# Four graph layers in a row: the middle product of the last three works on rows, with split operands, and every queue has a new order

## The chip, the core and the metric

The kernel runs on one core of a Trainium2 chip. A core has five engines that run side by side, each its own queue of instructions in a fixed order: TensorE (PE in the profile, with PEld for its weight loads), VectorE (DVE), ScalarE (ACT), GpSimd (POOL), and SyncE (SP), which here issues all transfers. They meet through semaphores: an instruction waits until a counter has reached a value that another engine's instruction raises. The metric is the time of one execution on the device in microseconds, as the median of several runs.

## The reference

The input is 128 small graphs of 128 nodes with 256 features each (`x`), and one weighted adjacency matrix of 128 x 128 for each (`adj`). Four blocks follow one another. Each takes `h = relu(layernorm(x))` and adds its result to `x`:

```python
x = x + L0(h, adj)   # hypergraph convolution 256 -> 512, relu, layer norm, 512 -> 256, residual
x = x + L1(h, adj)   # tanh(norm(adj) @ (h W) + b), with ones on the diagonal of adj != 0
x = x + L2(h, adj)   # attention: exp(leaky(8 tanh(score/8))) * adj, its sums, then (A h) w
x = x + L3(h, adj)   # three layers adj @ (x W) + b, relu after the first and the second
```

In L3, with A the adjacency matrix of one graph:

```python
x1 = relu(A @ (h  @ W1) + b1)
x2 = relu(A @ (x1 @ W2) + b2)
out =     A @ (x2 @ W3) + b3
```

Everything is computed in 32-bit precision or close to it. Since A @ (x W) = (A @ x) W, each layer may mix nodes first or weigh first.

## The kernel before, in words

**Streams and steps.** The 128 graphs go through in 16 groups of 4 streams (A, B, C, D) of J = 2 graphs each. Per stream and group there are the same steps, each named by block and kind. On PE a step `nU` ("unit") multiplies a graph's features with its 128 x 128 matrix, and a step `nW` ("weigh") multiplies with the layer's weights: `0U 0W 1U 1W` are L0, `2U 2W` L1, `3S 3U 3W` L2 (`3S` spreads the scores), and `4U 4W 5U 5W 6U 6W` L3. `G` forms the product of the incidence matrices.

**Two ways to multiply.** `unit` (L308) uses plain f32 products: the rows H (128 nodes x 256 features) are the stationary operand in two halves, the matrix of 128 x 128 moves through, so that the result lies in PSUM with features on the partitions, which is what the weighing needs as its stationary operand. There are two graphs and two halves, so four products of 128 x 128 a step; the trace counts each f32 product as two matmuls. `weigh` (L334) splits both operands in a high part rounded to fp32r and a low part (the rest), and adds three products, W low x U high, W high x U high, W high x U low: with 256 inputs and two graphs these are 12 fp32r matmuls, each of 256 moving columns.

**What the other engines do for one layer of L3.** After `4U`, ScalarE copies the bank rounded to fp32r (`take`, L435, tile UHI), VectorE subtracts that from the bank (`low`, L576, tile ULO), PE weighs (`4W`), VectorE adds the bias (`biased`, L618, tile H), ScalarE applies relu (`relu`, L483), and `5U` starts on H. `5U 5W` and `6U 6W` go the same way; `6W` ends in `last_out` on VectorE and a transfer.

**Around it.** GpSimd turns variances into scales (`norm`, L705 a power), prepares residuals, and in `with_loops` (step `AT`, L718 and L721) makes L1's matrix: incidences times a mask without diagonal, plus the identity. ScalarE's `normalise` (L404), `scores_tanh` (L470) and `scores_exp` (L477, L478), VectorE's `stats` (L535), `hidden` (L593), `leak`, `attend` and `attention_sums` (L624 to L635) serve the other blocks.

**PSUM.** Two wide pairs of banks serve `0W`, `1U` and the setup; four single banks serve all other PE steps in rotation. `bank_free` makes a step wait until the step four single-bank users earlier has been read by the engines named in `FREED`.

**Order.** The order of each queue is written out in full in `ORDER`, as three lists per engine: a first part, one turn that repeats, a last part. `ordered` numbers the occurrences of a step: the n-th is stream n modulo 4 and group n // 4. PE's turn has 16 steps; different steps of one turn belong to different streams, so that while one stream waits for ScalarE and VectorE the others keep PE at work. PE's first and last parts hold 73 and 72 steps. The SP queue loads and stores in the same manner: `T` loads the matrix for the next group once `6U` has read it, `R` the untransposed matrix, `O` stores a result.

## Time and profile before

| | |
|---|---|
| median of 3 runs | 1349.94 us (1349.46 to 1351.4) |
| the profiled execution | 1351.4 us |
| its span, first to last instruction | 1349.6 us |
| busy: PE, DVE, ACT, POOL | 1326.8, 1182.8, 1048.1, 1056.1 us |
| mean granted TensorE clock | 0.997 of full speed |
| DMA | 64.48 MB, 48 GB/s on the mean |

The span is shorter than the time of the execution by what lies before the first and behind the last instruction. Busy times are those of the profiled execution alone. A matmul's end is modelled and overlaps the start of the next; so a PE at 98% is one that is hardly ever without work, and what its work costs is better read from the distance between two starts. The same holds in a small measure for neighbours on ScalarE and VectorE.

### The profile page before, as it was taken

The numbers are of one execution on the slowest core, as the hardware profiler recorded it, in microseconds if no ns is written. First come the engines' busy times: TensorE is split into PE (matmuls) and PEld (weight loads), VectorE is DVE, ScalarE is ACT, GpSimd is POOL, SyncE is SP. The second block draws the span as 40 slices with busy tenths as digits, with TensorE's granted clock in tenths as the row PEclk, the third lists the DMA queues.
The fourth block names the chain that finished last, engine by engine and source line by source line (L and its number), as shares of the span: only waits on it lengthen the run. The fifth ranks groups of instructions, "written<-read, shape, count | busy, mean of one in ns | idle before, by whom it ended". The sixth has DMA issues, their size and how long they took to land.

```text
span 1349.6 us, 32286 instructions
## 1 busy us (share of the span) xinstructions
PE 1326.8 (98%) x10680; PEld 1282.2 (95%) x10680; DVE 1182.8 (88%) x3607; ACT 1048.1 (78%) x2632; POOL 1056.1 (78%) x2004
## 2 busy tenths in 40 slices
PE   8899999999999999999999999999999999999988
PEld 7889999999999999999999999999999999999987
DVE  8878898898998898898898898998998998989875
ACT  6776877887887887887887877877877877878864
POOL 7876778778788788788788788788788888888761
PEclk9989999999999999999999999999999999999999
DMA  7011111111111111111111111111111111111100
GB/s 215 21 32 33 44 57 37 48 56 37 48 56 37 48 56 37 48 56 37 48 56 37 48 56 36 49 53 39 49 50 39 52 48 37 56 48 33 33 9 32
DMA packets 83220, 64.48 MB, mean 48 GB/s; under 512 B 40304, under 2 KB 65520, under 8 KB 83056
## 3 DMA queue, kind: packets, MB, share of 16 engines
q1 hardware_dynamic: 83056, 62.43, 15.8%
q8 instruction: 87, 1.43, 0.4%
q14 instruction: 77, 0.63, 0.2%
HBM read 45.62 MB, written 16.78 MB: 46 GB/s over the span
## 4 chain that ended last, share of the span: by engine, by line
PE 89%; DVE 6%; ACT 2%; issue 1%; POOL 1%; DVEq 0%; POOLq 0%; ACTq 0%
PE BANK L351 29%; PE BANK L319 24%; PE BANK L358 14%; PE WIDE L330 8%; PE WIDE L351 8%; PE WIDE L358 4%; PE BANK L304 2%; PE BANK L369 1%; DVE BN_D L535 0%; DVE BN_B L535 0%; DVE BN_A L535 0%; DVE BN_C L535 0%; DVE ULO_B L576 0%; DVE ULO_A L576 0%; ACT H_B L404 0%
## 5 line engine op out<-in xcount | busy, mean ns | idle before, releaser
L576 DVE TENSOR_TENSOR ULO_D<-BANK,UHI_D 128x512 fp32r<-128x512 f32 x96 | 65.6, 684 | 18.6 <-ACT UHI_D L435 18.5
L576 DVE TENSOR_TENSOR ULO_B<-BANK,UHI_B 128x512 fp32r<-128x512 f32 x96 | 65.6, 683 | 17.5 <-ACT UHI_B L435 17.4
L576 DVE TENSOR_TENSOR ULO_A<-BANK,UHI_A 128x512 fp32r<-128x512 f32 x96 | 65.6, 683 | 17.0 <-ACT UHI_A L435 17.0
L576 DVE TENSOR_TENSOR ULO_C<-BANK,UHI_C 128x512 fp32r<-128x512 f32 x96 | 65.5, 683 | 14.1 <-ACT UHI_C L435 14.1
L435 ACT ACTIVATE UHI_C<-BANK 128x512 fp32r<-128x512 f32 x96 | 57.4, 598 | 21.3 <-PE BANK L319 20.1
L435 ACT ACTIVATE UHI_B<-BANK 128x512 fp32r<-128x512 f32 x96 | 57.3, 597 | 20.5 <-PE BANK L319 19.1
L435 ACT ACTIVATE UHI_A<-BANK 128x512 fp32r<-128x512 f32 x96 | 57.4, 598 | 19.5 <-PE BANK L319 18.1
L435 ACT ACTIVATE UHI_D<-BANK 128x512 fp32r<-128x512 f32 x96 | 57.3, 597 | 18.7 <-PE BANK L319 17.4
L705 POOL TENSOR_TENSOR LN_D<-LN_D,MHALF 128x2 f32<-128x2 f32 x80 | 55.7, 696 | 1.3
L705 POOL TENSOR_TENSOR LN_A<-LN_A,MHALF 128x2 f32<-128x2 f32 x80 | 55.7, 696 | 1.3
L705 POOL TENSOR_TENSOR LN_C<-LN_C,MHALF 128x2 f32<-128x2 f32 x80 | 55.6, 695 | 1.3
L705 POOL TENSOR_TENSOR LN_B<-LN_B,MHALF 128x2 f32<-128x2 f32 x80 | 55.6, 695 | 1.3
L404 ACT ACTIVATE H_B<-RES_B,LN_B 128x256 f32<-128x256 f32 x96 | 52.4, 600 | 5.1 <-POOL LN_B L713 5.0
L404 ACT ACTIVATE H_C<-RES_C,LN_C 128x256 f32<-128x256 f32 x96 | 52.4, 599 | 4.6 <-POOL LN_C L713 4.6
L404 ACT ACTIVATE H_A<-RES_A,LN_A 128x256 f32<-128x256 f32 x96 | 52.4, 599 | 3.9 <-POOL LN_A L713 3.9
L404 ACT ACTIVATE H_D<-RES_D,LN_D 128x256 f32<-128x256 f32 x96 | 52.3, 598 | 2.4 <-POOL LN_D L713 2.4
L319 PE MATMUL BANK<-T_B,H_B 128*128 128x128 f32 x384 | 51.7, 278 | 0.6 <-ACT H_B L483 0.6
L319 PE MATMUL BANK<-T_C,H_C 128*128 128x128 f32 x384 | 50.8, 275 | 0.5 <-ACT H_C L483 0.5
L319 PE MATMUL BANK<-T_A,H_A 128*128 128x128 f32 x384 | 50.7, 275 | 0.4 <-ACT H_A L483 0.4
L319 PE MATMUL BANK<-T_D,H_D 128*128 128x128 f32 x384 | 50.9, 275 | 0.2
L319 PEld LDWEIGHTS BANK<-T_B,H_B 128*128 128x128 f32 x384 | 48.6, 194 | 2.2 <-ACT H_B L483 0.8
L319 PEld LDWEIGHTS BANK<-T_D,H_D 128*128 128x128 f32 x384 | 47.8, 191 | 2.0 <-ACT H_D L483 0.7
(487 smaller groups left out, 5761.5 us busy)
## 6 DMA issues: line engine op xcount, KB each, us to landing
X_A<-in_xs SPq DMA_DIRECT2D x16, 256.0 KB, 2.5
X_B<-in_xs SPq DMA_DIRECT2D x16, 256.0 KB, 2.7
X_C<-in_xs SPq DMA_DIRECT2D x16, 256.0 KB, 2.6
X_D<-in_xs SPq DMA_DIRECT2D x16, 256.0 KB, 2.6
out_rows<-O_A SPq DMA_DIRECT2D x16, 256.0 KB, 2.0
out_rows<-O_B SPq DMA_DIRECT2D x16, 256.0 KB, 2.0
out_rows<-O_C SPq DMA_DIRECT2D x16, 256.0 KB, 2.1
out_rows<-O_D SPq DMA_DIRECT2D x16, 256.0 KB, 2.0
```

Of the source, the lines that this page charges most:

```text
L304: last = nc.tensor.matmul(bank(s, "G", k)[:, j * (P + 2):(j + 1) * (P + 2)], HT[s][:, j, :], BHT[s][:, j, :], start=True, stop=True)
L319: last = nc.tensor.matmul(bank(s, step, k)[:, at:at + P], lhs[s][:, j, m * P:(m + 1) * P], rhs(s, j), start=True, stop=True)
L330: last = nc.tensor.matmul(bank(s, "1U", k)[:, j, m * P:(m + 1) * P], Z[s][:, j, m * P:(m + 1) * P], GZ[s][:, j, :], start=True, stop=True)
L351: nc.tensor.matmul(dst, UHI[s][:, at[m]:at[m] + P], w[:, m, :], start=(w is lo and m == 0), stop=False)
L358: last = nc.tensor.matmul(dst, ULO[s][:, at[m]:at[m] + P], hi[:, m, :], start=False, stop=(m == chunks - 1))
L369: last = nc.tensor.transpose(bank(s, "3S", k)[:, j * P:(j + 1) * P], ST[s][:, S8, j:j + 1].to_broadcast([P, P]), IDENT[:, :])
L404: nc.scalar.activation(dst[s][:, j, :], src[s][:, j, :], ACT.Relu, bias=LN[s][:, NB, j:j + 1], scale=LN[s][:, RSTD, j:j + 1]).then_inc(sem ...
L435: nc.scalar.activation(UHI[s][:, 0:J * D], bank(s, step, k)[:, :], ACT.Copy).then_inc(sem(f"c{step}"), 1)
L576: nc.vector.tensor_tensor(ULO[s][:, 0:J * D], bank(s, step, k)[:, :], UHI[s][:, 0:J * D].bitcast(F32), ALU.subtract).then_inc(sem(f"l{step ...
L705: nc.gpsimd.tensor_tensor(rstd, ve, MHALF[:, :], ALU.pow)\
```

## The change

The middle layer of L3 now weighs first and mixes nodes afterwards; `4W` leaves its result with features on the partitions, so that `5W` can take it as the stationary operand without a `5U` in between.

- `4U` and its copy are laid out in pairs (`paired`): both graphs' columns side by side for each half of the features.
- `4W` is `weigh_columns`: the weights are stationary and 256 columns of UHI or ULO (two graphs x 128 nodes) move. 12 fp32r matmuls as before.
- ScalarE adds bias 1, now a column L3B1C, and applies relu in place in PSUM in two halves (`relu_columns`, step `4W`), then copies the bank to UHI (`take_columns`, step `4V`); VectorE subtracts (`low`, step `4V`).
- `5W` weighs with W2 from there; ScalarE copies and VectorE subtracts its result (steps `5W`).
- `5U` is `unit_rows`: the matrix T, split in THI and TLO, is stationary; the rows of UHI and ULO (256 columns) move. Per graph three fp32r matmuls, six in all. Then VectorE adds bias 2 (`biased`, step `5U`), ScalarE applies relu (`relu_rows`, step `5U`), and `6U`, `6W` are as before.
- THI is a rounded copy by ScalarE (`TH`), TLO the rest by GpSimd (`TL`).
- `with_loops` writes ones on the diagonal with two selections (`affine_select`) in place of a product and a sum; the mask OFFDIAG is gone.
- A user of a bank after `3S` also waits for `ae_ready`. The raw weights of `6W` have a tile of their own. Bias 1 is loaded as a column by one transfer, no longer spread over the partitions.
- All five orders are new, first and last parts too (left out below; PE's hold 73 and 72 steps again, and its turn is repeated 55 times in both kernels).

```diff
 ORDER = {
     "PE": (
...
-         "0U 4W 3S 0W 5U 2U 3U 5W 2W 3W G 6U 1U 1W 4U 6W",
...
+         "0U 4W 3S 0W 2U 5W 3U 2W 5U 3W G 6U 1U 1W 4U 6W",
...
     "ACT": (
...
-         "3W 2X 4U 2Y 0U 3T 4W 3E 1W SH 5U 2U 0W 3U R B 5W 2W 0Z H0 1U G 6U",
...
+         "G 1U 3W 2X TH 4U 2Y 0U SH 4W 4V 3T 1W 3E R 2U 0W 5W 3U B H0 5U 2W 0Z 6U",
...
     "DVE": (
...
-         "X XA 3L 3E 3R 0W 5U 2U 0S 3U 3I 0A 3J 5W 2W 3W 3S 3A 2S 2A 1U DA DB 6U T DC 1W 4U 1S DD 1A 0U 4W 6W",
...
+         "XA 4V 0W 3L 3E 3R 2U 0S 5W 3U 3I 0A 5U 2W 3J 3W 3S 3A 2S 2A 1U T DA DB X 6U DC 1W 1S 4U DD 1A 0U 6W",
...
     "POOL": (
...
-         "RX RB NZ 2A N3 N2 RH 2N DI AT N1 TB N0 X3",
...
+         "RB NZ 2A N3 N2 RH 2N AT TB N1 DI N0 RX TL X3",
...
     "SP": (
...
-         "W R F D O X T",
...
+         "D W O T F X R",
...
         B1 = sb("B1", [P, DH])
-        B2, L1B, L3B1, L3B2, L3B3 = (sb(n, [P, D]) for n in ("B2", "L1B", "L3B1", "L3B2", "L3B3"))
-        BIAS = {"4W": L3B1, "5W": L3B2}
+        B2, L1B, L3B2, L3B3 = (sb(n, [P, D]) for n in ("B2", "L1B", "L3B2", "L3B3"))
+        L3B1C = sb("L3B1C", [P, DC])
         BW = sb("BW", [P, D])
...
         IDENT = sb("IDENT", [P, P])
-        OFFDIAG = sb("OFFDIAG", [P, P])
         ONES = sb("ONES", [P, P])
...
         R = per_stream("R", J, P)
+
+        THI = per_stream("THI", J, P, dt=F32R)
+        TLO = per_stream("TLO", J, P, dt=F32R)
...
         L2WT = TMP["D"]
-        RAW = {"0W": W1, "1W": W2, "2W": O["A"], "3W": O["B"], "4W": O["C"], "5W": O["D"], "6W": H["D"]}
+        RAW = {"0W": W1, "1W": W2, "2W": O["A"], "3W": O["B"], "4W": O["C"], "5W": O["D"], "6W": sb("RAW6W", [P, DC, D])}
...
                 sp.dma_start(RAW[step][:, :, :], src).then_inc(sem(f"raw_loaded_{step}"), 16)
-            for dst, src in ((L1B, l1b), (L3B1, l3b1), (L3B2, l3b2), (L3B3, l3b3)):
+            for dst, src in ((L1B, l1b), (L3B2, l3b2), (L3B3, l3b3)):
                 sp.dma_start(dst[:, :], src.partition_broadcast(P)).then_inc(sem("bias_loaded"), 16)
+            column = bass.AP(l3b1.tensor, l3b1.offset, [[1, P], [P, DC], [1, 1]])
+            sp.dma_start(L3B1C[:, :].unsqueeze(2), column, allow_slow_non_contiguous=True).then_inc(sem("bias_column"), 16)
             for s in STREAMS[1:]:
...
             FREED = {"G": "cG", "3S": "sums_done", **{step: f"l{step}" for step in U_STEPS}, **{step: f"c{step}" for step in W_STEPS},
-                     "4W": "b4W", "5W": "b5W", "shifts": "w2c_ready"}
+                     "4W": "l4W", "5W": "l5W", "5U": "b5U", "shifts": "w2c_ready"}
             FREED_BY = {"c0W": J, "l1U": J, "c1W": J, "c2W": J, "c3W": J}
...
                     pe.wait_ge(sem(FREED[step0]), FREED_BY.get(FREED[step0], 1) * done_at(s0, k0))
+                    if step0 == "3S":
+                        pe.wait_ge(sem("ae_ready"), done_at(s0, k0))
...
-            def unit(step, lhs, rhs, *signals, rows=None):
+            def unit(step, lhs, rhs, *signals, rows=None, paired=False):
                 def f(s, c, k):
...
                         for m in range(DC):
-                            at = j * D + m * P
+                            at = (m * J + j) * P if paired else j * D + m * P
                             last = nc.tensor.matmul(bank(s, step, k)[:, at:at + P], lhs[s][:, j, m * P:(m + 1) * P], rhs(s, j),
...
-            def weigh(step):
+            def weigh_columns(s, c, k):
+
+                hi, lo = WHI["4W"], WLO["4W"]
+                if k == 0:
+                    pe.wait_ge(sem("weights_split"), W_STEPS.index("4W") + 1)
+                pe.wait_ge(sem("c4U"), c["n1"])
+                bank_free(s, "4W", k)
+                n = J * P
+                for q in range(DC):
+                    dst = bank(s, "4W", k)[:, q * n:(q + 1) * n]
+                    for w in (lo, hi):
+                        for m in range(DC):
+                            nc.tensor.matmul(dst, w[:, m, q * P:(q + 1) * P], UHI[s][:, m * n:(m + 1) * n],
+                                             start=(w is lo and m == 0), stop=False)
+                    if q == 0:
+                        pe.wait_ge(sem("l4U"), c["n1"])
+                    for m in range(DC):
+                        last = nc.tensor.matmul(dst, hi[:, m, q * P:(q + 1) * P], ULO[s][:, m * n:(m + 1) * n], start=False,
+                                                stop=(m == DC - 1))
+                last.then_inc(sem("p4W"), 1)
+
+            def unit_rows(s, c, k):
+
+                pe.wait_ge(sem("tl_ready"), c["n1"])
+                pe.wait_ge(sem("c5W"), c["n1"])
+                bank_free(s, "5U", k)
+                for j in range(J):
+                    dst, rows = bank(s, "5U", k)[:, j * D:(j + 1) * D], slice(j * D, (j + 1) * D)
+                    nc.tensor.matmul(dst, TLO[s][:, j, :], UHI[s][:, rows], start=True, stop=False)
+                    nc.tensor.matmul(dst, THI[s][:, j, :], UHI[s][:, rows], start=False, stop=False)
+                    if j == 0:
+                        pe.wait_ge(sem("l5W"), c["n1"])
+                    last = nc.tensor.matmul(dst, THI[s][:, j, :], ULO[s][:, rows], start=False, stop=True)
+                last.then_inc(sem("p5U"), 1)
+
+            def weigh(step, of=None, paired=False):
+                of = of or f"{step[0]}U"
                 chunks, n = WIDTH[step]
...
                         pe.wait_ge(sem("weights_split"), W_STEPS.index(step) + 1)
-                    pe.wait_ge(sem(f"c{step[0]}U"), c["v"][0] if step == "1W" else c["n1"])
+                    pe.wait_ge(sem(f"c{of}"), c["v"][0] if step == "1W" else c["n1"])
                     bank_free(s, step, k)
...
                         dst = to[:, j, :] if step == "0W" else to[:, j * n:(j + 1) * n]
-                        at = [j * chunks * P + m * P for m in range(chunks)]
+                        at = [(m * J + j if paired else j * chunks + m) * P for m in range(chunks)]
                         if step == "1W" and j:
...
                         elif j == 0:
-                            pe.wait_ge(sem(f"l{step[0]}U"), c["n1"])
+                            pe.wait_ge(sem(f"l{of}"), c["n1"])
                         for m in range(chunks):
...
                 "3U": unit("3U", H, lambda s, j: AE[s][:, j, :], "ae_ready"),
-                "4U": unit("4U", H, lambda s, j: T[s][:, j, :], rows="h3_ready"),
-                "5U": unit("5U", H, lambda s, j: T[s][:, j, :], "c4W"),
-                "6U": unit("6U", H, lambda s, j: T[s][:, j, :], "c5W"),
-                **{step: weigh(step) for step in W_STEPS}}
+                "4U": unit("4U", H, lambda s, j: T[s][:, j, :], rows="h3_ready", paired=True),
+                "5U": unit_rows,
+                "6U": unit("6U", H, lambda s, j: T[s][:, j, :], "c5U"),
+                **{step: weigh(step) for step in W_STEPS}, "4W": weigh_columns, "5W": weigh("5W", of="4W", paired=True)}
             run("PE", parts)
...
-            def relu(step):
-                def f(s, c, k):
-                    act.wait_ge(sem(f"b{step}"), c["n1"])
-                    nc.scalar.activation(H[s][:, :, :], H[s][:, :, :], ACT.Relu).then_inc(sem(f"c{step}"), 1)
-                return f
+            def relu_rows(s, c, k):
+                act.wait_ge(sem("b5U"), c["n1"])
+                nc.scalar.activation(H[s][:, :, :], H[s][:, :, :], ACT.Relu).then_inc(sem("c5U"), 1)
+
+            def relu_columns(s, c, k):
+
+                if k == 0:
+                    act.wait_ge(sem("bias_column"), 16)
+                act.wait_ge(sem("p4W"), c["n1"])
+                for q in range(DC):
+                    half = bank(s, "4W", k)[:, q * J * P:(q + 1) * J * P]
+                    last = nc.scalar.activation(half, half, ACT.Relu, bias=L3B1C[:, q:q + 1])
+                last.then_inc(sem("r4W"), 1)
+
+            def take_columns(s, c, k):
+                act.wait_ge(sem("r4W"), c["n1"])
+                nc.scalar.activation(UHI[s][:, 0:J * D], bank(s, "4W", k)[:, :], ACT.Copy).then_inc(sem("c4W"), 1)
+
+            def high_t(s, c, k):
+                act.wait_ge(sem("t_loaded", s), c["dma"])
+                nc.scalar.activation(THI[s][:, :, :], T[s][:, :, :], ACT.Copy).then_inc(sem("th_ready"), 1)
...
                      "2X": normalise(RES, H, "ln2_ready", "h2_ready"), "2Y": node_scores, "3T": scores_tanh, "3E": scores_exp,
-                     "3U": take("3U"), "3W": normalise(RES, H, "ln3_ready", "h3_ready"), "4U": take("4U"), "4W": relu("4W"),
-                     "5U": take("5U"), "5W": relu("5W"), "6U": take("6U")}
+                     "3U": take("3U"), "3W": normalise(RES, H, "ln3_ready", "h3_ready"), "4U": take("4U"), "4W": relu_columns,
+                     "4V": take_columns, "5W": take("5W"), "5U": relu_rows, "6U": take("6U"), "TH": high_t}
             run("ACT", parts)
...
                 if k == 0:
-                    dve.wait_ge(sem("bias_loaded"), 4 * 16)
+                    dve.wait_ge(sem("bias_loaded"), 3 * 16)
                 dve.wait_ge(sem("dinv"), c["n1"])
...
-            def biased(step):
-                def f(s, c, k):
-                    dve.wait_ge(sem(f"p{step}"), c["n1"])
-                    rows = bank(s, step, k)[:, :].rearrange("p (j d) -> p j d", j=J)
-                    nc.vector.tensor_tensor(H[s][:, :, :], rows, pair(BIAS[step][:, :]), ALU.add).then_inc(sem(f"b{step}"), 1)
-                return f
+            def biased(s, c, k):
+                dve.wait_ge(sem("p5U"), c["n1"])
+                rows = bank(s, "5U", k)[:, :].rearrange("p (j d) -> p j d", j=J)
+                nc.vector.tensor_tensor(H[s][:, :, :], rows, pair(L3B2[:, :]), ALU.add).then_inc(sem("b5U"), 1)
...
                      "3I": sums_inverse, "3J": sums_ratio, "3W": attention_out, "3S": stats(RES, "3", "c3W"),
-                     "3A": aggregate("3"), "4W": biased("4W"), "5W": biased("5W"), "6W": last_out, **{step: low(step) for step in U_STEPS}, "1U": low_hidden}
+                     "3A": aggregate("3"), "6W": last_out, **{step: low(step) for step in U_STEPS}, "1U": low_hidden, "4V": low("4W"), "5W": low("5W"),
+                     "5U": biased}
             dve.wait_ge(sem("ones_ready"), 1)
...
                                     pattern=[[-1, P]], channel_multiplier=1).then_inc(sem("ident_ready"), 1)
+            pool.wait_ge(sem("mhalf_ready"), 1)
             pool.wait_ge(sem("ident_ready"), 1)
-            nc.gpsimd.tensor_tensor(OFFDIAG[:, :], ONES[:, :], IDENT[:, :], ALU.subtract).then_inc(sem("offdiag_ready"), 1)
-            pool.wait_ge(sem("mhalf_ready"), 1)
-            pool.wait_ge(sem("offdiag_ready"), 1)
...
                 pool.wait_ge(sem("ht_ready"), c["n1"])
-                nc.gpsimd.tensor_tensor(AT[s][:, :, :], HT[s][:, :, :], pair(OFFDIAG[:, :]), ALU.mult)\
-                    .then_inc(sem("at_offdiag"), 1)
-                pool.wait_ge(sem("at_offdiag"), c["n1"])
-                nc.gpsimd.tensor_tensor(AT[s][:, :, :], AT[s][:, :, :], pair(IDENT[:, :]), ALU.add).then_inc(sem("at_ready"), 1)
+                for j in range(J):
+                    last = nc.gpsimd.affine_select(out=AT[s][:, j, :], in_=HT[s][:, j, :], compare_op=ALU.not_equal, fill=1.0, base=0,
+                                                   pattern=[[-1, P]], channel_multiplier=1)
+                last.then_inc(sem("at_ready"), 1)
...
+            def low_t(s, c, k):
+                pool.wait_ge(sem("th_ready"), c["n1"])
+                nc.gpsimd.tensor_tensor(TLO[s][:, :, :], T[s][:, :, :], THI[s][:, :, :].bitcast(F32), ALU.subtract)\
+                    .then_inc(sem("tl_ready"), 1)
+
             def last_bias(s, c, k):
                 if k == 0:
-                    pool.wait_ge(sem("bias_loaded"), 4 * 16)
+                    pool.wait_ge(sem("bias_loaded"), 3 * 16)
                 pool.wait_ge(sem("h3_ready"), c["v"][J - 1])
...
                      "NZ": norm("z"), "N1": norm("1", DINV), "2A": gcn_add, "N2": norm("2"), "2N": weighted, "N3": norm("3"),
-                     "X3": last_bias}
+                     "X3": last_bias, "TL": low_t}
             run("POOL", parts, per_pass=(1, 4))
```

## Rows read from the trace of the kernel before

**Rows 1.** The page's part 1: busy us of each engine, share of the span, instructions

```profile
PE 1326.8 (98%) x10680; PEld 1282.2 (95%) x10680; DVE 1182.8 (88%) x3607; ACT 1048.1 (78%) x2632; POOL 1056.1 (78%) x2004
```

**Rows 2.** Stretches; busy us of PE, weight loads, DVE, ACT, POOL; PE clock, DMA share, GB/s

```profile
65.00:70.00 5.00, 2.47 (x14) 2.26 (x13) 4.48 (x17) 4.39 (x12) 4.49 (x12) 0.78 0.00 0
...
80.00:85.00 5.00, 4.49 (x23) 4.30 (x24) 3.61 (x14) 3.68 (x10) 4.77 (x12) 0.66 0.02 3
...
sum 130.00, PE 118.01 PEld 109.99 DVE 106.06 ACT 88.92 POOL 97.58; mean PE 4.54 PEld 4.23 DVE 4.08 ACT 3.42 POOL 3.75
...
200.00:400.00 200.00, 200.00 (x1636) 194.58 (x1635) 180.64 (x552) 160.43 (x403) 162.61 (x308) 1.00 0.15 45
...
sum 130.00, PE 118.79 PEld 111.44 DVE 97.66 ACT 86.02 POOL 77.89; mean PE 4.57 PEld 4.29 DVE 3.76 ACT 3.31 POOL 3.00
```

**Rows 3.** The chain of waits, mid-body: start us, us, what

```profile
465.23 1.79 PE WIDE L330 x16
...
485.53 1.79 PE WIDE L330 x16
```

**Rows 4.** PE's timeline in one turn: start us, us, instructions

```profile
697.65 0.71 PE L351 MATMUL WIDE<-WLO0W,UHI_C 128*128 128x512 f32 x2
...
700.54 1.05 PE L319 MATMUL BANK<-T_D,H_D 128*128 128x128 f32 x8
701.43 1.06 PE L319 MATMUL BANK<-AT_B,H_B 128*128 128x128 f32 x8
702.32 1.06 PE L319 MATMUL BANK<-AE_A,H_A 128*128 128x128 f32 x8
703.13 0.48 PE L351 MATMUL BANK<-WLO5W,UHI_D 128*128 128x256 f32 x2
703.46 0.39 PE L351 MATMUL BANK<-WHI5W,UHI_D 128*128 128x256 f32 x2
...
704.59 0.39 PE L351 MATMUL BANK<-WLO2W,UHI_B 128*128 128x256 f32 x2
```

**Rows 5.** ScalarE's timeline in the same turn

```profile
698.51 0.63 ACT L483 ACTIVATE H_D<-H_D 128x512 f32<-128x512 f32 x1
699.03 0.39 ACT L477 ACTIVATE BANK<-AE_A 128x256 f32<-128x256 f32 x1
699.34 0.41 ACT L478 ACTIVATE AE_A<-AE_A 128x256 f32<-128x256 f32 x1
699.65 1.09 ACT L404 ACTIVATE H_B<-RES_B,LN_B 128x256 f32<-128x256 f32 x2
```

**Rows 6.** VectorE's timeline in the same turn

```profile
699.94 0.41 DVE L624 TENSOR_TENSOR BANK<-BANK,AE_A 128x256 f32<-128x256 f32 x1
...
701.21 1.41 DVE L593 SCALAR_TENSOR_TENSOR Z_C<-WIDE,ST_C,B 128x512 f32<-128x512 f32 x2
702.53 0.68 DVE L576 TENSOR_TENSOR ULO_D<-BANK,UHI_D 128x512 fp32r<-128x512 f32 x1
...
703.76 1.28 DVE L535 BATCH_NORM_STATS2 BN_C<-Z_C 128x6 f32<-128x512 f32 x2
```

**Rows 7.** Groups by line: busy us, mean ns of one, idle before them

```profile
L435 ACT ACTIVATE UHI_A<-BANK 128x512 fp32r<-128x512 f32 x96 | 57.4, 598 | 19.5 <-PE BANK L319 18.1
...
L618 DVE TENSOR_TENSOR H_A<-BANK,L3B 128x512 f32<-128x512 f32 x32 | 22.0, 689 | 4.0 <-PE BANK L358 3.2
...
L718 POOL TENSOR_TENSOR AT_A<-HT_A,OFFDIAG 128x256 f32<-128x256 f32 x16 | 11.7, 734 | 1.7 <-DVE HT_A L549 1.7
...
L687 POOL TENSOR_SCALAR_AFFINE_SELECT IDENT<-IDENT 128x128 f32<-128x128 f32 x1 | 0.3, 292 | 0.2 <-POOL IDENT L685 0.2
```

**Rows 8.** Timelines of ScalarE and PE in the last turns

```profile
1337.80 0.63 ACT L483 ACTIVATE H_C<-H_C 128x512 f32<-128x512 f32 x1 [0.73 <-DVE H_C L618]
...
1338.48 1.16 PE L319 MATMUL BANK<-T_C,H_C 128*128 128x128 f32 x8 [0.20 <-ACT H_C L483]
...
1344.31 0.50 PE L351 MATMUL BANK<-WLO6W,UHI_D 128*128 128x256 f32 x2 [0.69 <-ACT UHI_D L435]
```

55 rows, old and new, of the table ORDER are left out of this document.

## The prediction

> **What bounds the kernel now.** The page's first part comes first: TensorE (PE) is busy for 98% of the span, VectorE 88%, ScalarE and GpSimd 78% each [rows 1]. An average over stages says little, so the next view is the busy time of each engine by stretch. From 200 to 400 us PE is busy without a break, at the full granted clock (the 2.4 GHz level); in the same 200 us VectorE works 180.6, ScalarE 160.4 and GpSimd 162.6 [rows 2]. The idle time of PE lies at the two ends: 12.0 us in the first 130, 11.2 in the last 130. Two stretches of the beginning also show PE at a reduced clock, 0.78 and 0.66 on the mean of 5 us (part of each at the 1.2 GHz level), just after it had stood idle; that costs some (0.22 + 0.34) x 5 = 2.8 us. The third view is the chain of waits: in the middle it holds nothing but PE, and the same instruction comes back after 485.53 - 465.23 = 20.30 us [rows 3]. That is one turn of the written order, and the body repeats it 55 times before and 55 times after (64 less the `0U` written out in first and last part). So a microsecond taken from PE's turn is worth 55 to 64, and one taken from another engine nothing, as long as its results come in time.
>
> The fourth view is PE's timeline, and here start-to-start times count, not the mean of one: matmuls overlap in the pipeline, and the modelled 0.39 or 1.05 us of a group reaches into the next [rows 4].
>
> **The change, part by part.**
>
> *5U multiplies split operands (`unit_rows`).* Before, `5U` was four f32 products of 128 x 128, which the trace counts as 8 matmuls: 701.43 - 700.54 = 0.89 us [rows 4]. After, it is 6 fp32r matmuls that move 256 columns. Of a 5W's 12 such matmuls, the ten behind the first pair take 704.59 - 703.46 = 1.13, so one is 0.113 and six are 0.68. Gain 0.21 us. Passing from f32 to fp32r: the last f32 group before it takes 0.81 instead of 0.89 (702.32 to 703.13), the first pair 0.33 instead of 0.23, together 0.02 more. A turn has five such places before (ahead of 4W, 0W, 5W, 1W, 6W) and six after (2W now follows 3U), so 0.02 is lost. Net 0.19 a turn.
>
> The Trainium skill, "TensorE: Matmul & The Clock Gate", section "Back-to-back issue gap", gives a warm gap of N/2.4 + 2.5 ns, 109 ns at 256 columns. By that the six would take 0.66, and the sum below would be 1.6 us better. The rows' 113 decides here.
>
> *4W and 5W.* 4W keeps 12 matmuls with 256 moving columns; only which operand is stationary changes (`weigh_columns`). 5W keeps its 12. Cost nothing on PE: both forms load 128 columns of weights for 256 moving ones.
>
> *ScalarE.* Before, this layer pair took two relus of 128x512 (0.63 us each by their row) and the eviction of 5U; after: two halves of 128x256 with the bias (`relu_columns`), an eviction of them (`take_columns`), an eviction of 5W, one relu, and `TH`, a copy of 128x256. From start to start ScalarE needs 0.31 us for a 128x256, into PSUM or not (699.03, 699.34, 699.65), and 0.52 for a 128x512 (698.51) [rows 5]; I take that for the evictions too. Added: 2 x 0.31 + 0.52 + 0.31, removed one relu 0.52, and an estimated 0.1 for the wait on its own halves: +1.0 us a turn. By the full durations it is 2 x 0.39 + 0.60 + 0.41 - 0.63 = 1.16. ScalarE's load goes from 80% to about 85% of a turn; nothing on the path as long as it is below PE. A column bias read from PSUM back into PSUM is not in the trace: from below 0.31, from above the 0.60 of a full 128x512 eviction (598 ns, [rows 7]), so 0 to 0.6 us a turn more. I take 0.31, the row nearest in size.
>
> *VectorE.* Two bias additions (689 ns [rows 7]) and `5U`'s low part (0.68 us [rows 6]) become the low parts of 4W and 5W and one bias addition: the same count at the same price, 0.
>
> *GpSimd.* `with_loops` loses two operations of 128x256 (734 ns and its like), and gains two selections of 128x128. One selection of that size took 0.3 us, 292 ns, in the setup [rows 7]. `TL` adds one subtraction of 128x256, 0.73. Sum: 0.58 + 0.73 - 1.47 = -0.15; if a selection costs as much as the 734 of a whole pair, +0.73. GpSimd has 19% free. Covered; 0. Loading a bias as a column (256 small pieces) is one DMA in place of a broadcast, needed only at the first 4W, some 70 us in: 0.
>
> *The new places in the order.* Do results still come in time? I lay one turn of the new PE order against the queues, time 0 at the end of 0W, which takes 700.54 - 697.65 = 2.89 [rows 4]. PE: 4W ends at -3.0, 2U 0.9, 5W 2.3, 3U 3.2, 2W 4.6, then 5U to 5.3, 3W to 6.6, G, 6U from 7.1. ScalarE from -2.9: 4W, 4V, 3T, 1W, 3E, R, 2U, 0W, 5W, nine parts of 0.5 to 1.0, some 6.0 in all: its take of 5W is done at 3.1. VectorE: second half of 0W until 0.7 (a pair takes 1.32 [rows 6]), leak, attend and sums 1.27 (699.94 to 701.21), low 2U 0.61 (two lows: 702.53 to 703.76), then 0S 1.2, low 5W: done near 4.4. 5U wants that low part only after its first two matmuls, at 4.8: 0.4 to spare. Its bias and relu end near 6.6 for a 6U at 7.1: 0.5 to spare. The narrowest is 6U's bank, freed by VectorE's 2W at about 6.85: 0.25. All positive, so the turn stays PE's and is 20.30 - 0.19 = 20.11.
>
> *The last turns.* Before, PE waits at the end for pairs of bias and relu: from the start of ScalarE's relu to the dependent 5U are 1338.48 - 1337.80 = 0.68, and the last 6W starts 0.69 after PE fell idle [rows 8]; with the low parts some 2.2 us are lost in the last 14. In the new order D's 6U still waits for bias and relu (1.6 less C's 6U, 0.89: 0.7 us), while C's 6W covers the take before D's 6W. That is 1.5 better; I take 1.0. For the beginning I find no reason of either sign and take 0: bounds are -8 (idle and slow clock there, less what the first loads need) and +6 (another wait with a slow stretch behind it). The tail's bounds are -5 and +4.
>
> **Sum.** 64 x 0.19 = 12.2, plus 1.0: span 1349.6 - 13.2 = 1336.4. The profiled execution took 1351.4, 1.8 more than its span; so 1338.2. The median of the runs is 1.46 below the profiled one, so **1336.7 us**.
>
> **Rivals.**
> - *A queue becomes late in each turn* (slower side). Place: the low part of 5W or the release of 6U's bank. Speaking for it: three queues are now 81 to 91% full, each in fixed order, and the slack found above is 0.25 to 0.5 us; a column relu at the 0.60 bound eats 0.6 of ScalarE's. Against: ScalarE is not the latest of the two at 5U (3.1 against 4.4), and before, with VectorE just as full, PE never waited. A wait of w costs 55w: at w = 0.24 all is gone, at 0.35 the time is 1336.7 + 19 = 1356. Chance of slower 0.08, of within the noise 0.08, of a small wait that leaves a gain (1342) 0.08.
> - *The new order mends the ends*: half of the idle and slow time at both ends goes, 6 us more: 1331. For it: every list of the first part is new, and setup work on VectorE is placed later. Against: new waits on ScalarE there. Chance 0.12.
> - *The ends get worse* by 5: 1342. For it: PE stood idle, and then ran at the lower level, after a single late result; ScalarE has 1 us more per stream. Chance 0.08.
> - *The split product isn't cheaper*: if each of the six had to wait for its own weights for longer than it runs, 0.19 us each where PE's own pace is 0.113 (an estimate: nearest above is the f32 product's 0.22, four in 0.89), 5U would be 1.13, 0.26 worse than before a turn: 1366. Against: 5W's twelve load as often and start every 0.113. Chance 0.01.
> - The forecast itself, 1333 to 1341: 0.55.
>
> A difference of 0.2% (2.7 us) is what a measurement of this kernel can tell from none. Faster: 0.55 + 0.12 + 0.08 + 0.08 = 0.83; within: 0.08; slower 0.09. Range 1329 to 1346.
>
> **What would show it.** A turn of 20.1 us in the chain of waits and PE busy without a break from 200 to 1200; six fp32r matmuls of `unit_rows` in 0.68; the relu halves near 0.39; PE's list of waits without VectorE's ULO or H in the middle. Wrong would be: a turn of 20.3 or more, with idle time before 5U or 6U, or clearly more idle time than 12.0 and 11.2 us in the first and the last 130.

## The result, and the profile after

The changed kernel takes 1375.85 us (median, 1375.02 to 1376.55) against 1350.67 (1349.46 to 1354.02) for the kernel before on the same chip: ratio 1.0182, 95% interval 1.0168 to 1.0196. It is slower; the forecast was 1336.7. Its profiled span is 1373.2 us against 1349.6.

Part 1 of the page after, in the columns of [rows 1]:

```profile
PE 1348.1 (98%) x10552; PEld 1293.4 (94%) x10552; DVE 1202.0 (88%) x3607; ACT 1112.6 (81%) x2824; POOL 1037.1 (76%) x2067
```

PE has 128 instructions fewer and 21.3 us more of busy time. ScalarE gained 64.5 us, about what was forecast, GpSimd lost 19, twice the forecast, and neither is full. The stretches that answer to [rows 2], same columns (stretch, its length, then the busy times):

```profile
0.00:130.00 130.00, 117.59 (x822) 108.92 (x823) 102.04 (x320) 92.91 (x228) 92.34 (x196) 0.97 0.25 72
200.00:400.00 200.00, 199.60 (x1590) 192.72 (x1590) 180.25 (x545) 165.18 (x421) 154.89 (x308) 1.00 0.16 46
1243.20:1373.20 130.00, 119.20 (x936) 113.14 (x934) 101.67 (x285) 93.35 (x233) 80.09 (x157) 1.00 0.11 33
```

The ends are as before (118.01 and 118.79 of PE there), and in the middle PE still looks full at the full clock. Busy time does not show the loss: modelled ends of matmuls overlap and cover short waits. The chain of waits does. The rows that answer to [rows 3] are the same matmuls of `0W`, one turn apart:

```profile
401.71 0.93 PE WIDE L394 x4
...
422.44 0.93 PE WIDE L394 x4
```

A turn takes 20.73 us instead of 20.30. With the 55 turns of the body this is nearly the whole loss: from the first turn's start to the last one's end there are 1140.9 us, before 1118.1, so +22.8. The first part is 2.5 longer, the last 1.7 shorter.

To see which step of the turn grew, I took the time from each step's first matmul to the next step's first, median over the turns between 200 and 1200 us (microseconds; "6U" is followed by `1U` in both kernels; e3 to e15 are experiments told below; steps that hardly moved are left out):

| step | before | after | e3 | e6 | e14 | e15 |
|---|---|---|---|---|---|---|
| 6W | 1.503 | **1.802** | 1.511 | 1.498 | 1.498 | 1.458 |
| 1W | 2.848 | 2.919 | 2.957 | 2.931 | 2.933 | 2.934 |
| 4W | 1.462 | 1.520 | 1.519 | 1.499 | 1.497 | 1.468 |
| 5W | 1.456 | 1.495 | 1.495 | 1.460 | 1.460 | 1.460 |
| 3W | 1.362 | 1.413 | 1.413 | 1.382 | 1.418 | 1.418 |
| 2W | 1.360 | 1.513 | 1.512 | 1.499 | 1.500 | 1.501 |
| 6U | 0.891 | 0.929 | 0.929 | 0.959 | 0.925 | 0.891 |
| 5U | 0.892 | 0.700 | 0.700 | 0.724 | 0.692 | 0.692 |
| 2U | 0.893 | 0.809 | 0.808 | 0.809 | 0.809 | 0.809 |

(`2U` and `2W` belong together: `2U` now stands ahead of fp32r matmuls and so ends 0.08 sooner, `2W` stands behind f32 ones and starts 0.10 slower; that is the passage of the forecast, 0.02 net.) 5U gave its 0.19. Two things ate it: **6W waits** 0.30 a turn, and **each step of 256-column matmuls is slower**, 0.27 a turn in all: 1W 0.07, 2W with 2U 0.05 net of the passage, 3W 0.05, 4W 0.06, 5W 0.04. With 0.04 at 6U and 0.02 for the passage: -0.19 + 0.30 + 0.27 + 0.04 + 0.02 = +0.44.

**The wait.** PE's timeline of the kernel after, in one turn (start us, us):

```profile
708.27 0.48 PE L394 MATMUL BANK<-WLO6W,UHI_C 128*128 128x256 f32 x2
708.59 0.39 PE L394 MATMUL BANK<-WHI6W,UHI_C 128*128 128x256 f32 x2
709.03 0.50 PE L401 MATMUL BANK<-WHI6W,ULO_C 128*128 128x256 f32 x2
709.37 0.40 PE L394 MATMUL BANK<-WLO6W,UHI_C 128*128 128x256 f32 x2
```

VectorE's, just ahead of that. `DA` (L615, L616) and `DB` (L621) prepare node degrees and their inverses, on two elements each, `X` (L594) is the statistics of the input, and L635 is the low part of `6U`:

```profile
706.43 1.09 DVE L615 TENSOR_SCALAR ST_C<-G_C 128x2 f32<-128x2 f32 x1
707.44 0.15 DVE L616 SCALAR_TENSOR_TENSOR ST_C<-DIAG_C,G_C 128x2 f32<-128x2 f32 x1
707.56 0.17 DVE L621 RECIPROCAL ST_C<-ST_C 128x2 f32<-128x2 f32 x1
707.64 0.75 DVE L594 BATCH_NORM_STATS2 BN_D<-X_D 128x6 f32<-128x256 f32 x2
708.31 0.68 DVE L635 TENSOR_TENSOR ULO_C<-BANK,UHI_C 128x512 fp32r<-128x512 f32 x1
```

And GpSimd's:

```profile
706.20 1.29 POOL L806 TENSOR_TENSOR RES_B<-RES_B,H_B 128x512 f32<-128x512 f32 x1
```

From the second to the third PE row are 0.44 instead of 0.23: the low part of `6U` lands at 708.99. The pair behind it takes 0.34 instead of 0.23 as well; together 0.32, which is the 0.30 of the table in this turn. That low part stands on VectorE behind `T DA DB X`, and `DA`'s first operation, on two elements, takes 1.09 us where it took 0.18 to 0.24 before. It began while GpSimd's addition of two SBUF tiles ran (706.20 to 707.49) and ended 0.03 behind it. The group of one stream in the kernel before (busy us, mean ns | idle before them), the slowest of the four:

```profile
L556 DVE TENSOR_SCALAR ST_C<-G_C 128x2 f32<-128x2 f32 x16 | 3.8, 237 | 0.0
```

and in the kernel after, where the other three streams have 856 to 970 ns:

```profile
L615 DVE TENSOR_SCALAR ST_D<-G_D 128x2 f32<-128x2 f32 x16 | 15.6, 973 | 0.0
```

That agrees with the Trainium skill, "SBUF — State Buffer", section "Who interferes with whom": a `tensor_scalar` of VectorE can take the port pair that it shares with GpSimd, an exclusive lock, and whoever comes second is blocked for the other's whole instruction.

The kernel before had the same two operations side by side and did not pay, because there `DA` came first (VectorE's timeline, then GpSimd's):

```profile
711.88 0.19 DVE L556 TENSOR_SCALAR ST_D<-G_D 128x2 f32<-128x2 f32 x1
...
711.99 1.30 POOL L750 TENSOR_TENSOR RES_C<-RES_C,H_C 128x512 f32<-128x512 f32 x1
```

In the turns between 200 and 1200 us the kernel before starts `DA` 0.11 us ahead of that addition (median); the changed kernel starts it 0.24 us behind the addition's start. With this shift of 0.35 us `DA` went from 0.18 to 1.09.

**The pace.** In [rows 4] the pairs of a 5W start every 0.225 us, 113 ns a matmul. In the kernel after, nearly every 256-column fp32r matmul takes 115 to 120 in a fixed pattern (median by position in `3W`: 117, 115, 118, 117, 120; single positions of `2W` and `4W` reach 123 and 125). Ten of a `3W`, 1.17 us:

```profile
720.75 0.40 PE L394 MATMUL BANK<-WLO3W,UHI_A 128*128 128x256 f32 x2
...
721.92 0.40 PE L401 MATMUL BANK<-WHI3W,ULO_A 128*128 128x256 f32 x2
```

The f32 matmuls (112) did not change, the 512-column ones hardly (233 before, 234 after). Nothing about most of these steps was edited. What moved were addresses: `L3B1C`, 8 bytes wide, takes 32 of each partition, so `UHI` and `ULO` stand 224 bytes above a multiple of 512, before 192, while the weights stayed at 128 (all places below are bytes modulo 512, as the built program lays the tiles out). So in most steps the stationary tile stood 64 above the moving one before, and stands 96 above it after.

### The profile page after: what moved, and what is told of

It reads as the page before. It is cut to its first block, busy times and chain, and to the rows that moved or that the text cites. A ratio compares the mean times of both kernels' runs of the same rounds, so it can differ in the third digit from the quotient of the medians.

```text
span 1373.2 us, 32422 instructions
## 1 busy us (share of the span) xinstructions
PE 1348.1 (98%) x10552; PEld 1293.4 (94%) x10552; DVE 1202.0 (88%) x3607; ACT 1112.6 (81%) x2824; POOL 1037.1 (76%) x2067
## 4 chain that ended last, share of the span: by engine, by line
PE 83%; DVE 10%; issue 3%; ACT 3%; POOL 1%; DVEq 0%; POOLq 0%; ACTq 0%
PE BANK L394 20%; PE BANK L326 18%; PE BANK L401 12%; PE WIDE L394 8%; PE WIDE L337 8%; PE BANK L353 4%; PE WIDE L401 4%; PE BANK L358 2%; PE BANK L311 2%; PE BANK L370 1%; PE BANK L373 1%; PE BANK L369 1%; PE BANK L412 1%; DVE BN_B L594 1%; DVE ST_A L615 1%
## 5 line engine op out<-in xcount | busy, mean ns | idle before, releaser
L635 DVE TENSOR_TENSOR ULO_C<-BANK,UHI_C 128x512 fp32r<-128x512 f32 x112 | 76.5, 683 | 25.0 <-ACT UHI_C L539 15.8
L635 DVE TENSOR_TENSOR ULO_D<-BANK,UHI_D 128x512 fp32r<-128x512 f32 x112 | 76.4, 682 | 24.1 <-ACT UHI_D L539 13.0
L635 DVE TENSOR_TENSOR ULO_A<-BANK,UHI_A 128x512 fp32r<-128x512 f32 x112 | 76.5, 683 | 23.2 <-ACT UHI_A L539 11.8
L635 DVE TENSOR_TENSOR ULO_B<-BANK,UHI_B 128x512 fp32r<-128x512 f32 x112 | 76.5, 683 | 21.0 <-ACT UHI_B L539 12.3
L757 POOL TENSOR_TENSOR LN_B<-MV_B,EPS 128x2 f32<-128x2 f32 x80 | 15.6, 195 | 55.0 <-DVE MV_B L602 54.9
L534 ACT ACTIVATE BANK<-BANK,L3B1C 128x256 f32<-128x256 f32 x128 | 51.9, 443 | 5.9 <-PE BANK L358 3.1
L757 POOL TENSOR_TENSOR LN_A<-MV_A,EPS 128x2 f32<-128x2 f32 x80 | 15.6, 195 | 49.9 <-DVE MV_A L602 49.9
L757 POOL TENSOR_TENSOR LN_C<-MV_C,EPS 128x2 f32<-128x2 f32 x80 | 15.6, 195 | 48.8 <-DVE MV_C L602 48.8
L757 POOL TENSOR_TENSOR LN_D<-MV_D,EPS 128x2 f32<-128x2 f32 x80 | 15.6, 195 | 47.7 <-DVE MV_D L602 47.7
L594 DVE BATCH_NORM_STATS2 BN_A<-RES_A 128x6 f32<-128x256 f32 x96 | 35.6, 411 | 1.5 <-POOL RES_A L811 1.5
```

What stands on the lines that cost most here:

```text
L534: last = nc.scalar.activation(half, half, ACT.Relu, bias=L3B1C[:, q:q + 1])
L594: last = nc.vector.bn_stats(BN[s][:, j, :], src[s][:, j, :])
L635: nc.vector.tensor_tensor(ULO[s][:, 0:J * D], bank(s, step, k)[:, :], UHI[s][:, 0:J * D].bitcast(F32), ALU.subtract).then_inc(sem(f"l{step ...
L757: nc.gpsimd.tensor_tensor(ve, MV[s][:, :, 1], EPS[:, :], ALU.add).then_inc(sem("ve" + tag), 1)
```

## Experiments

Two theories after the result. *Wait*: 6W is late because 6U's low part is behind `DA`, which GpSimd holds up. *Pace*: placement of tiles sets how fast 256-column matmuls run. The rival to each is the other, and that the new forms (columns, split 5U) are slow in themselves. Ratios are to the kernel before, on the same chip. The runs come from several chips, on which the kernel before takes 1348.1 to 1350.7, so medians of different rows compare to within some 2 us.

| run | median us (range) | ratio [95%] | before, same chip |
|---|---|---|---|
| e1 | 1376.27 (1375.69–1377.01) | 1.0192 [1.0177, 1.0207] | 1350.17 |
| e2 | 1367.48 (1365.62–1369.57) | 1.0127 [1.0109, 1.0145] | 1350.17 |
| e3 | 1360.27 (1359.87–1360.44) | 1.0073 [1.0058, 1.0088] | 1350.17 |
| e4 | 1367.98 (1367.37–1368.41) | 1.0129 [1.0112, 1.0146] | 1350.17 |
| e5 | 1371.45 (1371.27–1372.02) | 1.0165 [1.0149, 1.0180] | 1349.47 |
| e6 | 1354.27 (1354.12–1354.95) | 1.0038 [1.0024, 1.0052] | 1349.47 |
| e7 | 1370.12 (1368.18–1372.51) | 1.0155 [1.0136, 1.0174] | 1349.47 |
| e8 | 1360.71 (1360.59–1363.89) | 1.0090 [1.0075, 1.0105] | 1349.47 |
| e9 | 1351.83 (1351.23–1353.13) | 1.0023 [1.0013, 1.0033] | 1348.09 |
| e10 | 1368.49 (1364.63–1368.95) | 1.0137 [1.0119, 1.0156] | 1348.09 |
| e11 | 1354.81 (1354.22–1355.32) | 1.0042 [1.0027, 1.0057] | 1348.09 |
| e12 | 1369.64 (1367.51–1370.43) | 1.0146 [1.0133, 1.0160] | 1349.44 |
| e13 | 1372.31 (1370.26–1374.56) | 1.0174 [1.0157, 1.0192] | 1349.44 |
| e14 | 1352.29 (1351.62–1353.03) | 1.0023 [1.0014, 1.0032] | 1349.44 |
| e15 | 1349.16 (1348.32–1349.53) | 0.9997 [0.9987, 1.0007] | 1349.85 |

**e3, the changed kernel with `6U` ahead of `T DA`.** VectorE's turn:

```
-... 2S 2A 1U T DA DB X 6U DC 1W 1S 4U DD 1A 0U 6W
+... 2S 2A 1U 6U T DA DB X DC 1W 1S 4U DD 1A 0U 6W
```

> The changed kernel with one move in VectorE's turn: the low part of 6U stands ahead of T, DA, DB and X instead of behind them. Theory C (a late low part): 6W waits 0.3 us a turn for ULO because DA, a two-element operation, stands still for 0.9 us ahead of it, during a long GpSimd operation. With the low part ahead of it the 6W block falls from 1.80 to 1.50 us a turn, and the time to 1376 - 16 = 1360. Rival: another result is late right behind it (1W's eviction, 1S, the low of 4U), and the time moves by under 4 us. The pace of the matmuls stays at 117 to 120.

16 us came back: 6W fell from 1.802 to 1.511, and of the other steps only 1W moved, by +0.04. The wait was worth 16 of the 25 us. `DA` now takes about 0.49 (median), since it starts 0.83 behind the start of GpSimd's addition.

**e4, `DA`'s first operation in the form that also writes out an accumulator**, orders unchanged.

```
-tensor_scalar(ST[s][:, DNM, :], DNS[s], TINY, None, ALU.max)
+tensor_scalar(ST[s][:, DNM, :], DNS[s], TINY, 0.0, ALU.max, ALU.add, accum_out=SPARE[:, :])
```

> The changed kernel with DA's first operation (the maximum with TINY, 128x2) in the form that also writes its sum to a spare element; order unchanged. Theory D (lock): that operation took a median of 1.09 us against 0.18 before because its plain form can't run beside GpSimd's long addition (RES_B, 1.29 us), and ends when that ends; the form with a sum, which T uses beside GpSimd at 0.28, isn't held up. Then it takes 0.2 to 0.3 us, 6W's wait goes and the time is near 1360. Rival: any operation in this place waits (for the data of G or for the diagonal), it stays near 1 us, and the time at 1376.

Half of e3's 16 us came back (-7.9, 6W at 1.625): neither the 1360 of the theory nor the 1376 of the rival. VectorE's timeline in e4:

```profile
702.67 0.15 DVE L616 TENSOR_SCALAR_CACHE_REDUCE ST_C<-G_C 128x2 f32<-128x2 f32 x1
...
702.75 1.00 DVE L618 SCALAR_TENSOR_TENSOR ST_C<-DIAG_C,G_C 128x2 f32<-128x2 f32 x1
703.68 0.15 DVE L623 RECIPROCAL ST_C<-ST_C 128x2 f32<-128x2 f32 x1
```

GpSimd's in e4:

```profile
702.45 1.29 POOL L808 TENSOR_TENSOR RES_B<-RES_B,H_B 128x512 f32<-128x512 f32 x1
```

The first operation takes 0.15 as the theory says, and the hold moved to the next, which reads two SBUF tiles: 1.00 us for two elements, ending with GpSimd's. What was won is that the held operation is now the last of `DA`'s two: `DB` starts 0.06 before the addition ends (703.68), after the change it started 0.07 behind that (707.56), and 0.13 times 55 is 7 us. So the loss is the meeting of these two engines, not an operation's own cost; the cure is order, not form. That the form with the accumulator goes free and the one with two SBUF inputs does not agrees with the same section of the Trainium skill.

**e1, e2, e7, e8: a pad of 32, 64 or 128 bytes ahead of the working tiles**, in the changed kernel (e1: `UHI` at 256) and in the kernel before (e2, e7, e8: 224, 256, 320).

```
+        PAD = sb("PAD", [P, 8])      # e1, e2;  16 in e7, 32 in e8
```

> The changed kernel with an unused tile of 32 bytes behind L3B1C, so that every tile behind it starts at a multiple of 64 bytes again, as before the change; nothing else differs. Theory A (placement): fp32r matmuls of 256 columns start 117 to 120 ns apart in the changed kernel and 113 before because UHI and ULO now start 32 bytes off such a multiple. Then the pace goes back to 113 to 114, a turn loses about 0.3 us, and the time is 1376 - 19 = 1357 us. Rival B (load): the pace comes from fuller neighbours (ScalarE in PSUM, the split T) or from later signals; then it stays at 117 to 120 and the time at 1376.

> The kernel before with the same unused tile of 32 bytes ahead of BW, so that all tiles behind the biases, UHI and ULO among them, start 32 bytes off a multiple of 64; order and work are those of before. Theory A: the pace of the 256-column fp32r matmuls goes from 113 to 117 or more and the time to 1350 + 17 = 1367 us. Rival B: 113 and 1350 stay.

> The kernel before with an unused tile of 64 bytes ahead of BW: UHI_A at 256 modulo 512, as in the changed kernel with its 32-byte pad, still a multiple of 64. Theory A2: the pace rises to 117 to 120, the time to about 1366, as with 32 bytes. Rival A1 (only starts off a multiple of 64 are slow, and in the changed kernel something else kept the pace down): 113 and 1350 us.

> The kernel before with an unused tile of 128 bytes ahead of BW: UHI_A at 320 modulo 512, the same modulo 128 as in the kernel before. If the offset counts modulo 128, the pace stays at 113 and the time at 1350 us; if modulo 256 or 512, the pace rises to 117 or more and the time to about 1366.

e2 is the clean one: the kernel before, with one unused tile more, loses 17 us. e1 was to take 1357 and stayed at 1376. In e1 and e7 `UHI` is at a multiple of 64 again and nothing is mended, so that theory of mine fell; in e8 all these steps run at an even 118.

**e10, the kernel before with only `UHI` and `ULO` 32 bytes on** (a pad in front, one of 480 behind, so the rest is where it was modulo 512).

```
+        PAD = sb("PAD", [P, 8])
         UHI = per_stream("UHI", J * DH, dt=F32R)
         ULO = per_stream("ULO", J * DH, dt=F32R)
+        PAD2 = sb("PAD2", [P, 120])
```

> The kernel before with only UHI and ULO, the tiles TensorE reads in all W steps, 32 bytes further on; every other tile is where it was modulo 512. Theory A (the pace is set between the two operands of a matmul): as when all tiles moved by 32 (1367.5), matmuls of 256 columns at 115 to 120 ns, +17 on before. Theory B (it is the tiles of the other engines, which meet TensorE's reads or each other): within 3 of before's 1350.

As slow as e2. So the pace hangs on where TensorE's own operands lie, not on other engines' tiles. Its timeline in a 4W, eight matmuls in 0.95 us, 119 ns each:

```profile
705.66 0.40 PE L353 MATMUL BANK<-WHI4W,UHI_D 128*128 128x256 f32 x2
...
706.61 0.40 PE L360 MATMUL BANK<-WHI4W,ULO_D 128*128 128x256 f32 x2
```

**e12, e13, the kernel before with the weights 32 or 64 bytes on**, everything else at its place modulo 512.

```
+        PAD = sb("PAD", [P, 8])       # 16 in e13
         WHI = {...}; WLO = {...}
+        PAD2 = sb("PAD2", [P, 120])   # 112 in e13
```

> The kernel before with the split weights 32 bytes further on, and all tiles behind them where they were modulo 512: UHI and ULO stand 32 above the weights modulo 512, not 64. So far 64 gave 1350 (113 ns), 96 gave 1367, 128 gave 1370, 192 gave 1361 (all at 115 to 122). Theory A (the distance between the two operands of a matmul sets the pace): another value than 1350 is possible, within 1350 to 1370; if 96 is slow because it is no multiple of 64, so is 32 (1367). Theory C (the absolute place of UHI sets it, 192 is good): 1350, since UHI has not moved.

> The same with the weights 64 bytes further on, so that UHI, ULO and the weights all stand at 192 modulo 512. Theory A with growing distance as the harm (64 better than 96, 128, 192): not slower than 1350, the 118 ns of 6W also down to 113, at best 1345. Theory A with 64 as the one good distance: 1360 to 1370. Theory C (absolute place of UHI): 1350.

`UHI` did not move and the pace broke: 116 to 122 in e12, an even 120 in e13. So the place of `UHI` alone does not decide: moving either operand breaks the pace. By distance of `UHI` above the weights, modulo 512, the kernel before takes: 0: 1372, 32: 1370, **64: 1349**, 96: 1367, 128: 1370, 192: 1361. 64 is the one good distance of the six tried; the others don't stand in order of size.

That it is the distance, and not the pair of places, is not shown: no run moved both operands together and kept 64. And distance is not all. The two operands of the new `5U` stand 128 apart in the kernel after, in e1, e5 and e6 alike, at different places, and `5U` took 0.700, 0.717, 0.724 and 0.724.

**e5, e6: the changed kernel with the distance of 64 given back**, the bias column put in a spare end of an existing tile (e5), and that with e3's order (e6).

```
-        COLS = sb("COLS", [P, 2 * HC + DC])
-        L3B1C = sb("L3B1C", [P, DC])
+        COLS = sb("COLS", [P, 2 * HC + 2 * DC])
+        L3B1C = COLS[:, 2 * HC + DC:]
```

> The changed kernel with the column bias in the spare end of the tile COLS in place of a tile of its own; every tile behind it moves down by 32 bytes, so that UHI, ULO and all working tiles lie at the same offsets modulo 512 bytes as in the kernel before (UHI_A at 192, where it is 224 in the changed kernel and 256 with the 32-byte pad), while the weights WHI and WLO stay where they were. Theory A2 (placement matters, but not as a multiple of 64: what counts is the offset of the working tiles against the weights): 256-column fp32r matmuls are back at 113 to 114 ns, the time at 1376 - 19 = 1357 us. Rival B: in the changed kernel's mix the pace is 117 to 120 whatever the placement, and the time stays at 1376.

> The same with the low part of 6U ahead of T, DA, DB and X on VectorE. If both causes are real and independent, 1376 - 16 - 19 = 1341 us, faster than the kernel before, with a turn near 20.1 us. If placement does nothing here, 1360. If the faster matmuls only uncover another late result, in between.

e5 gave 4.4 us by the medians and only 2.3 by the ratios, whose intervals overlap with the changed kernel's; 19 were expected. e6 gave 22 in all and took 1354 where 1341 was expected if both causes were independent. In e5 part of what the even pace gave back was lost again at 6U (0.96) and 5U (0.72). In e6 steps run at either of two even paces, 113 or 118: 3W always at 113, 4W at 118, and for 1W, 2W, 5W and 6W it changes from turn to turn. In the kernel before nearly all run at 113 and only 6W at 118.

**e9, e11: is it the distance in the new forms, or a longer period?** e9 puts the halves of `T` and the weights of 4W 64 above what they are multiplied with; e11 makes all places equal to before's modulo 1024.

```
# e9
+        MONE, MHALF = ...                     # two 32-byte places: from here offset 256
+        WHI["4W"], WLO["4W"], THI, TLO = ...  # moved here
+        LEAST, EPS = ...
# e11
-        ONES = sb("ONES", [P, P])   # now behind the last tile
```

> Base is e6 (span 1352.3, turn 20.39). Only addresses change: the halves of T (stationary in 5U) and the weights of 4W (stationary in the column form) now stand 64 bytes above the tile they are multiplied with, modulo 512, as UHI stands above the weights in the kernel before; in e6 they stood 128 above and 64 below. Theory A (what counts is how far the stationary tile stands above the moving one, and 64 gives 113 ns a matmul): 5U 0.724 -> 0.68 and 4W 1.499 -> 1.46, turn -0.08, total -5 to 1349. Theory B (what counts is only whether the moving or stationary tile stands at 192, or the step's neighbours): 5U and 4W as in e6, total 1354 within 1.

> Base is e6 (span 1352.3). ONES (512 bytes) now stands behind all tiles, so each tile in front of which it stood lies where before's does modulo 1024 instead of only modulo 512. If distance modulo 1024 (a row of 256 fp32r columns) sets which of the two paces, 113 or 118 ns, a step takes: 1W 2.93 -> 2.85, 2W 1.50 -> 1.46, turn -0.12 or more, total about 1347. If only modulo 512 counts: 1354 within 1, and the choice of pace depends on something else (the order of steps, their phase).

5U went from 0.724 to 0.692 (0.68 was expected), the total by 2.4 of the 5 expected. 4W hardly moved: its median stayed (1.497), 14 of its 49 turns fell to 113 or 114, while 3W, untouched, went to 118 in about half of the turns. So e9 speaks for the distance in 5U and not clearly in 4W. Places equal modulo 1024 (e11) change nothing, 1354.8 against 1354.3.

**e14, e15: the last short wait.** 6U still took 0.03 to 0.07 too long. e14 (on e9) moves VectorE's `0A` (statistics for `1U`) ahead of `3U 3I`, to have `1U`'s matrix `GZ` earlier; e15 (on e14) takes `2W` on VectorE in one operation, which frees 6U's bank earlier. e15 leaves out the scaling of L1's sum by the inverse degree, so its result is not that of the reference; only its timing is of use.

```
-... 2U 0S 5W 3U 3I 0A 5U 2W ...
+... 2U 0S 5W 0A 3U 3I 5U 2W ...                                    # e14
-for j: scalar_tensor_tensor(TMP_j, bank_j, DINV_j, L1B, mult, add)
+tensor_tensor(TMP, bank, pair(L1B), add)                           # e15
```

> Base is e9 (1351.8; its 1U waits 0.05 us a turn for GZ, whose statistics 0A stand on VectorE behind 3U's low part and 3I). Only edit: 0A ahead of 3U and 3I in VectorE's turn. If that wait is a queue's lateness: T to 1U 0.943 -> 0.89, -0.05 a turn, -3 to about 1349 (ratio to before 1.000 within 0.001). If the time is lost again at 3W (low part of 3U now 0.1 later) or to another pace: 1352.

> Base is e14 (1352.3), whose earlier 0A changed nothing: GZ was not what delays TensorE at 6U. The profile shows there H's relu ended 0.24 us before 6U and VectorE's 2W, which frees 6U's bank, 0.12 us before. Here VectorE takes 2W in one addition of 128x512 (about 0.61 from start to start) instead of two operations of 128x256 (0.79); this leaves out the scaling of the graph convolution's sum. Theory A (the bank is what 6U waits for): T to 1U 0.943 -> 0.89, -3 us. Theory B (A, and the short wait in each turn is also what throws TensorE from the pace of 113 ns into that of 118 about every second time): the paces of 2W, 3W, 5W become the same in all turns, a further -0.1 to -0.2 a turn, -8 to -12 in all. Neither: 1352.

e14 changed nothing: `GZ` was the wrong suspect. e15 did what theory A of its expectation said: 6U back at 0.891, -3.1 us. It also starts all that stands behind `2W` on VectorE sooner; what points at the bank is that the lost time lay between 6U's first and second matmul (144 ns in e14, 109 in e15). PE's timeline in e14, `6U` and the step behind it, 0.92 from one start to the other:

```profile
609.31 1.09 PE L327 MATMUL BANK<-T_C,H_C 128*128 128x128 f32 x8
610.23 0.72 PE L338 MATMUL WIDE<-GZ_B,Z_B 128*128 128x128 f32 x5
```

The same in e15, 0.89:

```profile
607.73 1.05 PE L327 MATMUL BANK<-T_C,H_C 128*128 128x128 f32 x8
608.62 1.95 PE L338 MATMUL WIDE<-GZ_B,Z_B 128*128 128x128 f32 x16
```

Theory B came half true. Without the wait most steps keep one pace in nearly every turn (5W and 6W 113 to 114, 1W, 2W and 3W 118; 4W by stream), where in e14 they changed from turn to turn. But they settled as much on 118 as on 113, so nothing further was won. How the slower of the two paces is entered stays open.

No version found beats the kernel before. e9 and e14 are the best complete ones, 0.2% behind; e15 is level with it and leaves work out.

## Why the prediction was wrong

Two steps failed: the price of the matmuls that were thought unchanged, and the walk through the turn.

- *What bounds the kernel* was right: PE, in the turn. All but 0.8 of the 23.6 us more of span lie in the body.
- *5U from 0.89 to 0.68*: nearly right, 0.70 (0.113 a matmul taken, 0.117 measured).
- *4W and 5W keep their 12 matmuls each, "Cost nothing on PE"*: **failed**. The count stayed, the pace didn't. I carried 0.113 over as a constant of the instruction, from rows of one placement; it is also a matter of where its two operands lie. The eight bytes of `L3B1C` were priced as "one DMA"; their place in SBUF was not priced at all. Cost: 0.27 a turn. Only part of it is placement in the narrow sense: the same 32 bytes cost the kernel before 17 us (e2), but giving the distance back gave the changed one 4.4 (after to e5) and 6.0 (e3 to e6), and 2.4 more in the new forms (e9). The rest is that the changed kernel runs many steps at the second pace, 118, even at the good distance, and for that no cause is shown: the new order, the new forms and the short wait at 6U changed together.
- *The walk of the turn, "All positive"*: **failed in two places**. The one at 6W was not walked: I checked 5U, 6U's `H` and 6U's bank and left out 6U's low part, which the change puts behind `T DA DB X` on VectorE, before it was behind `DA DB`. With `DA` at its old 0.24 it would have come 0.85 earlier, at 708.14, before it was wanted (708.82), so the second half of the miss was to price `DA` from its own rows without asking what GpSimd does at its new moment. e3 and e4 show both halves. The one at 6U's bank was walked, with 0.25 of slack; it was in truth some 0.04 late (e14 against e15).
- *ScalarE +1.0 to 1.16, GpSimd -0.15*: right in size for ScalarE (+64 us over 64 turns: 1.0); GpSimd's -19 us, or -0.3 a turn, is twice the forecast. Their load as such cost nothing, but the moment of one GpSimd operation did. The halves take 0.44, between the bounds.
- *Ends*: the last part is 1.7 better, 1.0 was forecast, and as it was forecast: D's 6U still waits, the last 6W (1368.30) no longer does, where it waited 0.69 in [rows 8]; the first is 2.5 worse, within the bounds. PE's timeline after, the row that answers to those:

```profile
1365.88 1.16 PE L326 MATMUL BANK<-T_D,H_D 128*128 128x128 f32 x8 [0.55 <-ACT H_D L525]
...
1368.30 0.40 PE L394 MATMUL BANK<-WLO6W,UHI_D 128*128 128x256 f32 x2
```

- The rival *a queue becomes late in each turn* is what happened in part, with w = 0.30 at 6U's low part ahead of 6W, a place it did not name, 0.04 at the bank and nothing at 5W's low part. I gave it 0.08 for a slower kernel, because the kernel before never waited; that says nothing of slack in a new order. The second cause had no rival at all.
- The 109 ns at 256 columns that the forecast cites from the Trainium skill, "TensorE: Matmul & The Clock Gate", section "Back-to-back issue gap", lies below both paces, 113 and 118. The page gives it for a single matmul by itself, not for a stream with weight loads, which the forecast did not say; nothing hung on it.

## To carry over

When a change adds or removes a tile, however small, print the places of the tiles that TensorE reads, stationary and moving, and keep both where they are; a pad is the control experiment, and it should be run before a change of order is judged. When steps are moved in a fixed queue, walk every result that PE waits for, and look at what the other of VectorE and GpSimd does at the new moment: a two-element operation cost 1 us here. Compare start-to-start times by step; busy shares showed neither loss.
